# Score matmuls of the retention heads on four 32-column tiles instead of one of 128 columns

## What is computed

```
retention = jnp.einsum('mhsd,mhtd->mhst', q, k) * decay      # decay = 1 / (1 + |s - t|)
out = jnp.einsum('mhst,mhtd->mhsd', retention, v) + k
```

## Time and profile before

| | us |
|---|---|
| median of 3 runs | 8461.63 |
| lowest and highest | 8458.88, 8468.84 |
| span of the profiled execution, first to last instruction | 8460.6 |
| retention heads in it, first to last score step of DVE | 6090.0 to 8192.7 |
| busy time over the whole program: PE, DVE, ACT, POOL | 7417.9 (88%), 4769.0 (56%), 3185.4 (38%), 2338.1 (28%) |

### The profile page before, as it was taken

The page is one execution under the profiler, slowest core; times in us unless marked ns, Lnnn a source line. Parts: engine busy times, 40 slices in busy tenths (PEclk is TensorE's granted clock), DMA queues, the critical chain, the costliest instruction groups (busy, mean ns, idle before and its releaser), DMA issues. The chain is left out here.

```text
span 8460.6 us, 164061 instructions
## 1 busy us (share of the span) xinstructions
PE 7417.9 (88%) x53035; PEld 3625.5 (43%) x53035; DVE 4769.0 (56%) x7714; ACT 3185.4 (38%) x5336; POOL 2338.1 (28%) x2558
## 2 busy tenths in 40 slices
PE   6799999999996775799999970997799999999987
PEld 4233333333333552576666760775433333333326
DVE  6777777777772401232232243114677777777766
ACT  2166666666663241222222210212444444444432
POOL 0011111111111000000000003002388888888861
PEclk8699999999998786899999965998899999999986
DMA  4211111111114314000000031114611111111113
GB/s 118 58 33 33 33 33 33 33 33 33 33 29 95 104 46 132 27 13 13 26 1 17 1 119 54 52 49 135 200 31 30 30 31 29 30 30 31 30 50 105
DMA packets 414311, 426.01 MB, mean 50 GB/s; under 512 B 76199, under 2 KB 386635, under 8 KB 408590
## 3 DMA queue, kind: packets, MB, share of 16 engines
q1 hardware_dynamic: 331790, 339.52, 14.2%
q0 software_dynamic: 62400, 59.16, 2.8%
q10 hardware_dynamic: 19712, 21.53, 0.8%
HBM read 253.37 MB, written 166.55 MB: 50 GB/s over the span
## 5 line engine op out<-in xcount | busy, mean ns | idle before, releaser
L624 DVE TENSOR_REDUCE softmax_part_max<-softmax_ring 128x1 f32<-128x512 f32 (+1 forms) x2880 | 1727.2, 634 | 494.0 <-PE softmax_ring L534 464.0
L2421 DVE TENSOR_TENSOR retention_decayed<-retention_scores,retention_decay_table 128x768 f32<-128x768 f32 x1728 | 1655.4, 958 | 475.0 <-PE retention_scores L2381 475.0
L2440 POOL TENSOR_TENSOR retention_decayed<-retention_third,retention_decay_table 128x384 f32<-128x384 f32 x1728 | 1723.4, 997 | 456.7 <-ACT retention_third L2462 415.5
L664 ACT ACTIVATE softmax_probs<-softmax_scores 128x768 f32<-128x768 f32 x1728 | 1399.2, 811 | 885.8 <-PE softmax_scores L553 847.3
L2462 ACT COPY retention_third<-retention_scores 128x384 f32<-128x384 f32 x1728 | 827.9, 479 | 1276.6 <-PE retention_scores L2381 1276.6
L534 PE MATMUL softmax_ring<-softmax_k_next,softmax_q_next 96*128 96x512 bf16 (+1 forms) x2880 | 1086.5, 379 | 139.7 <-DVE softmax_part_max L624 49.7
L2394 PE MATMUL retention_sums<-retention_decayed,retention_v_piece 128*32 128x288 f32 x13824 | 1197.8, 418 | 0.5 <-POOL retention_decayed L2440 0.5
L2381 PE MATMUL retention_scores<-retention_q_half,retention_k_piece 96*128 96x384 bf16 x5184 | 1145.7, 330 | 29.4 <-DMA retention_v_piece<-ret_v 29.3
L565 PE MATMUL softmax_sums<-softmax_probs,softmax_v_piece 128*32 128x192 f32 x13824 | 930.2, 343 | 0.6 <-ACT softmax_result L653 0.5
L553 PE MATMUL softmax_scores<-softmax_q_third,softmax_k_piece 99*128 99x384 bf16 x3456 | 870.8, 333 | 5.9 <-ACT softmax_probs L664 5.9
L2381 PEld LDWEIGHTS retention_scores<-retention_q_half,retention_k_piece 96*128 96x128 bf16 x5184 | 366.6, 98 | 947.2 <-issue 832.2
(11 more groups left out here) (299 smaller groups left out, 6483.4 us busy)
## 6 DMA issues: line engine op xcount, KB each, us to landing
ret_v<-ret_proj_values SPq DMA_DIRECT2D x8, 1728.0 KB, 8.8
retention_v_piece<-ret_v SPq DMA_DIRECT2D x144, 96.0 KB
softmax_q_third<-rope_q SPq DMA_DIRECT2D x192, 54.0 KB
softmax_q_next<-rope_q POOLq DMA_DIRECT2D x64, 162.0 KB, 3.9
softmax_k_piece<-rope_k SPq DMA_DIRECT2D x192, 54.0 KB
softmax_k_next<-rope_k POOLq DMA_DIRECT2D x64, 162.0 KB, 5.5
ret_q<-ret_proj_parts SPq DMA_DIRECT2D x48, 216.0 KB
ret_k<-ret_proj_parts SPq DMA_DIRECT2D x48, 216.0 KB
```

What stands on the lines that cost most here:

```text
L624: nc.vector.reduce_max(part_max[:, j, c:c + 1], ring[m % 2][:, 0:CHUNKS[c][1]], axis=X)\
L664: nc.scalar.activation(probs[n % 4][:, :].rearrange("p (c q) -> p c q", c=2), scores[n % 2][:, :, 0:QC], ACT.Exp, scale=scale).then_inc(ex ...
L2421: nc.vector.tensor_tensor(weights[n % 4][:, 0:2 * QC].rearrange("p (c q) -> p c q", c=2), scores[n % 2][:, 0:2, 0:QC], table[:, table_at(n ...
L2440: nc.gpsimd.tensor_tensor(weights[n % 4][:, 2 * QC:HALF], third[n % 3][:, :], table[:, at:at + QC], ALU.mult)\
```

## The change

Each score matmul of 128 keys becomes four of 32 keys. The weight of each is a 96x32 piece of the same key tile, and each writes to its own 32 partitions of the same bank. The queries that are moved through are the same 96x384 for all four. The order is third by third (`c`), and within a third the four groups of keys (`g`). What is computed, the tiles in PSUM, the semaphores and all other engines' code stay as they were. A step has 12 score matmuls and 12 weight loads where it had 3 of each; the value matmuls stay.

```diff
                 for c in range(3):
-                    last = nc.tensor.matmul(scores[n % 2][:, c, 0:QC],
-                                            k_piece[t // PT][:, t % PT * P:(t % PT + 1) * P],
-                                            q_half[half][:, c * QC:(c + 1) * QC], start=True, stop=True)
+                    for g in range(4):
+                        at = t % PT * P + 32 * g
+                        last = nc.tensor.matmul(scores[n % 2][32 * g:32 * g + 32, c, 0:QC], k_piece[t // PT][:, at:at + 32],
+                                                q_half[half][:, c * QC:(c + 1) * QC], start=True, stop=True)
                 last.then_inc(scored, 1)
```

## The result

The changed kernel takes 8067.64 us (median of 4 runs, 8064.76 to 8075.42), the kernel before 8461.74 beside it. The ratio is 0.9535 with a 95% interval of 0.9521 to 0.9548. The direction was forecast; the size was not, and the time lies 82 us under the low end of the range. The profiled execution has a span of 8073.9 us, for 8460.6 before.

A forecast was written before the change was run, and what follows sets the result against it. PE was taken to set retention's 1.2175 us step; two gaps gone (0.20 less) and costlier score rounds (0.07 more) gave 1.093, 215 us less over 1728 steps: 8461.6 to 8247 us, range 8150 to 8330, chance 0.62.

The forecast's parts named there:

- step 1: PE's retention step: with all matmuls on 32-column tiles both 0.10 us gaps between 128 and 32 columns go, 0.20 less.
- step 2: Retention scores: three matmuls become three rounds of four at 0.187 us, 0.561 in place of 0.49, 0.07 more a step.
- step 4: Sum for PE's retention step: 2 x 0.266 + 3 x 0.187 = 1.093 us for 1.2175, over 1728 steps 215 us less.
- lower bound of 1.041: Retention step with score rounds of 0.163 us: 0.532 + 0.489 + 0.02 = 1.041, which is 305 us less.
- step 3: Score weight loads, 12 of 32 columns for 3 of 128: hidden within a round, costed at nothing; exposed, 0.3 us a step.
- step 5: Other engines in retention: POOL's 0.997 and DVE's 0.958 us are below 1.04; transfers and semaphore waits add nothing.
- half the gap stays: Upper end of the forecast's own range, 8330 us, for retention on PE keeping half the gap.
- A: PE's retention loop body, grown to 1440, refetches code at each of 46 branches: 300 us more, 8547; chance 0.20.
- B: PE's gap belongs to the change between bf16 and f32 and stays: step 1.280 us, 108 more, 8569; chance 0.07.
- C: Four bf16 score streams don't run at full rate side by side: step 1.573 us, 9076, or about 10,660; chance 0.06.
- D: PE's instruction supply limits retention: at 33 matmuls and loads a us, step 1.21 and time unchanged, about 8461; chance 0.05.
- The tells: Retention signs: step 1.09 us, DVE's idle 0.26 to 0.13, POOL's 0.22 to 0.09, branch near 0.21, clock 1.00, other stages unmoved.

The follow-up runs named there:

- 64-column kernel: Changed kernel with retention's score matmuls on two tiles of 64 columns instead of four of 32, values still on 32: 8478.6 us, step 1.231.
- bf16 kernel: Kernel before the change with the value matmuls in bf16 too, scores still on 128 columns: 8836.5 us, 368 slower than the kernel before beside it.
- 1842: Changed kernel with four more one-column score matmuls a step, PE's loop body growing from 1554 to 1842 instructions: 8401.4 us, branch 3607 ns.

## Why the prediction was right in direction and short by 179 us

- **Both gaps go (step 1): right.** 0.20 a step was forecast, and no gap stands in the step any more. That f32 and bf16 still alternate without one, and the 64-column kernel, settle that the change of tiling is its cause.
- **The rounds of four (step 2, and the sum in step 4): this is the step that failed.** The prediction took 0.187 for a round from the softmax heads and 0.266 for a value round, and read the 0.027 above streaming as a price of every round of four. Both had been read at the same place, the first interval of a group just behind a change of tiling. Without a change value rounds are 0.24 apart and score rounds 0.16 to 0.17. The terms were 3 x 0.187 + 2 x 0.266 = 1.093; measured is 0.49 + 0.48, which is 0.977 over 33 steps. That is 0.116 a step, 200 us; less the 28 at the edges it is 172 of the 179 that are missing. Even the lower bound of 1.041 kept 0.266 for the values and 0.02 for a stagger, so the range's low end was too high. The 128-column scores in the earlier trace rows already had the pattern, with 0.17 for the first interval and 0.16 for the second. That the first weight load behind a change has nothing to hide under is the likeliest cause of the 0.027: it starts with its matmul there, and 0.20 ahead of it in the changed kernel. No run tests it by itself.
- **Weight loads (step 3): right, hidden.** A load of 96x32 takes 94 ns (median) beside rounds of 0.16, and the twelve of a step leave no mark. The reading behind it was off in two places, without effect: the 128x32 load of 106 to 109 ns in the earlier trace rows is longer than the 98 of the 128-column one, not "no longer", and not all eight loads of a value group lay under running matmuls, since the first started with its own.
- **What is late next (step 5): right for 1.093, nearly wrong for 0.977.** DVE's 0.958 is below it by 19 ns. POOL's 0.997 an operation is above it, yet it keeps up, because its operations start every 0.964 at best and overlap in the records. Had it started one only every 0.997, the stage would have stopped there. The first two of the earlier trace rows, 1.94 for both, had shown this.
- **The edges:** 0.59 us a head, 28 us, had no term; before, no such excess stood out.
- **The range's upper bound:** 8330 was to be "half the gap stays", but it counts half of one gap (0.05 x 1728 = 86 us). Half of both is 0.10 a step, 173 us, and 8420. It played no part in the outcome.
- **The rivals.** A was not met, and it is real: 288 instructions more would have brought it. B (type) fell to the bf16 kernel. C fell to the score rounds of 0.16, four bf16 streams side by side at full rate. D would have held PE at 33 matmuls and loads a us; it does 40. The Trainium skill, page "TensorEngine Tiling (Array Packing)", section "Tiling Modes", says that changing the tiling mode drains the engine and changing the tile doesn't. The traces agree, with 0.12 and 0.09 at the changes between 128 and 32 columns, 0.11 and 0.09 between 64 and 32, and none from one 32-column tile to the next. That column tiling and fast weight load exclude each other (the same page of the Trainium skill, "Restrictions and Gotchas") had no price to be seen here, by the 94 ns above.
- **The tells.** DVE's and POOL's idle time was to fall to 0.13 and 0.09 a step; it fell to 0.05 and 0.06 (89.9 and 102.9 us over 1728). The branch stayed at 208 ns and the clock at 1.00, as forecast, and no other stage moved.

## What to carry to other kernels

Where matmuls of different tile widths alternate, price each change of width: here 0.12 us into the scores and 0.09 out of them, beside up to 0.03 in the first round behind it. Then give all of them one width, since converting part of a group can add changes (the scores alone in softmax: 314 us lost against the changed kernel). Take the price of a round from an interval with the same tiling ahead of it, not from the first of a group. Before a loop is made longer, count the instructions of its body: at 1842 most of this change's gain was lost to fetching code.

## What was not expected of the hardware

- **Less work on PE left it at half the clock.** With bf16 values a step holds less streaming, and the granted clock stayed at 0.50 for the whole stage of 1728 steps, with PE recorded busy for 100.00 of 100.00 us. The step was 1.433 for an expected 0.98. No run tells why the clock stayed there. In the kernel before and the changed one the stage begins at the same level (0.53 in the 30 us ahead of it) and is at 1.00 within the first steps (0.97 over the first 100 us). A share of busy time near 100% thus says nothing of the clock.
- **Matmuls are started past a waiting one** if their own tile is free: four within 34 ns, though three matmuls of one tile stand together in the code.
- **Four loads and four matmuls of one column cost 0.03 us a step**, so issuing a load and a matmul takes at most some 7 ns. Issue is not what limits the changed kernel to its 40 a us.
